# A gated linear attention layer and a channel-mixing layer on eight cores: one subtraction moved from VectorE to GpSimd, and three weight loads moved behind the first tile of phase B

## The reference

```python
# layer 1: a linear attention with a data-dependent decay
h = layernorm(x)
q = silu(h @ Wq.T);  f = sigmoid(h @ Wk.T);  v = h @ Wv.T
log_f = log_sigmoid(f);  k = 1 - f                      # 8 heads of 128
S_t = exp(log_f_t)[:, None] * S_{t-1} + k_t[:, None] * v_t[None, :]
o_t = q_t @ S_t
x = x + layernorm(rmsnorm(o, norm_w) @ Wo.T)
# layer 2: token shift, then a gated feed-forward
h = layernorm(x);  hp = h shifted by one token
xr = mu_r*h + (1-mu_r)*hp;  xk = mu_k*h + (1-mu_k)*hp
x = x + layernorm(sigmoid(xr @ W_r) * (square(relu(xk @ W_k)) @ W_v))
```

## Time and profile before

| | us |
|---|---|
| median of 2 runs | 5861.55 (5776.55 and 5946.55) |
| the profiled execution | 5770.28 |
| its span on core 1, the slowest | 5768.7 |
| spans of the 8 cores | 5745.9 to 5768.7 |

### The profile page before, as it was taken

The page is one execution under the profiler, slowest core; times in us unless marked ns, Lnnn a source line. Parts: engine busy times, 40 slices in busy tenths (PEclk is TensorE's granted clock), DMA queues, the critical chain, the costliest instruction groups (busy, mean ns, idle before and its releaser), DMA issues.

```text
span 5768.7 us, 65821 instructions; the slowest of 8 cores (5745.9 to 5768.7 us)
## 1 busy us (share of the span) xinstructions
PE 3475.0 (60%) x26608; PEld 2614.8 (45%) x26608; DVE 1992.9 (35%) x1978; ACT 1060.8 (18%) x1597; POOL 448.2 (8%) x205
## 2 busy tenths in 40 slices
PE   0566666666666666662056667666567666656665
PEld 0344444444444444441044455544445554444554
DVE  1333333333333333344123323333332323333233
ACT  0222222222222222221011111111111111111110
POOL 1111101100100111111310000000000000000000
PEclk9877777777777777776578888888778887778887
DMA  2000000000000000001210000000000000000000
GB/s 81 26 14 14 15 15 15 15 15 15 15 15 15 15 15 15 15 8 44 76 33 15 23 23 1 23 23 22 23 22 23 1 23 23 23 23 23 23 6 10
DMA packets 114736, 121.83 MB, mean 21 GB/s; under 512 B 3683, under 2 KB 107270, under 8 KB 114438
## 3 DMA queue, kind: packets, MB, share of 16 engines
q1 hardware_dynamic: 114438, 117.63, 6.5%
HBM read 83.00 MB, written 34.62 MB: 20 GB/s over the span
## 4 chain that ended last, share of the span: by engine, by line
PE 53%; DVE 26%; ACT 7%; DMA 6%; issue 5%; POOL 3%; DVEq 1%; ACTq 0%; POOLq 0%; SPq 0%
PE p_pj L250 39%; PE p_st L231 4%; PE p_pj L400 4%; DVE b_sb L329 3%; PE p_O L514 1%; PE p_O L531 1%; DVE r_a L207 1%; DMA outT<-x_sb 1%; ACT ebq L361 1%; DMA oB<-o_scr 1%; DVE p_A L457 1%; PE p_A L479 1%; DVE A_l L462 1%; DVE A_h L460 1%; POOL ebk L349 1%
## 5 line engine op out<-in xcount | busy, mean ns | idle before, releaser
L250 PE MATMUL p_pj<-o_pair,woh 128*128 128x256 bf16 x2176 | 414.6, 298 | 537.8 <-POOL o_pair L763 310.6
L250 PEld LDWEIGHTS p_pj<-o_pair,woh 128*128 128x128 bf16 x2176 | 228.7, 106 | 596.4 <-issue 553.2
L231 PE MATMUL p_st<-x_sb,onesc 128*1 128x256 f32 x544 | 172.2, 487 | 473.1 <-ACT oB L897 268.8
L250 PE MATMUL p_pj<-ln_h,wkh 128*128 128x256 bf16 x1088 | 311.9, 287 | 199.3 <-DVE ln_l L613 199.3
L250 PE MATMUL p_pj<-xk_h,wv2h 128*128 128x256 bf16 x1088 | 309.6, 285 | 125.0 <-DVE xk_l L821 125.0
L250 PE MATMUL p_pj<-o_pair,wol 128*128 128x256 bf16 x1088 | 322.3, 296 | 0.0
L231 PEld LDWEIGHTS p_st<-x_sb,onesc 128*1 128x1 f32 x544 | 53.3, 101 | 591.1 <-issue 560.3
L250 PE MATMUL p_pj<-xr_h,wrh 128*128 128x256 bf16 x1088 | 297.7, 274 | 24.8 <-DVE xk_l L938 24.8
L250 PE MATMUL p_pj<-ln_l,wkh 128*128 128x256 bf16 x1088 | 311.7, 287 | 0.0
L250 PE MATMUL p_pj<-ln_h,wkl 128*128 128x256 bf16 x1088 | 310.7, 286 | 0.0
L250 PE MATMUL p_pj<-xk_l,wv2h 128*128 128x256 bf16 x1088 | 309.7, 285 | 0.0
(11 more groups left out here) (176 smaller groups left out, 7903.5 us busy)
## 6 DMA issues: line engine op xcount, KB each, us to landing
x_sb<-xT SPq DMA_DIRECT2D x17, 1024.0 KB, 5.3
o_scr<-o_stage SPq DMA_DIRECT2D x68, 256.0 KB, 2.3
oB<-o_scr SPq DMA_DIRECT2D x17, 1024.0 KB, 5.4
xB<-xT SPq DMA_DIRECT2D x17, 1024.0 KB, 5.3
outT<-x_sb SPq DMA_DIRECT2D x16, 1024.0 KB, 4.5
wstage<-wkT SPq DMA_DIRECT2D x8, 512.0 KB
wstage<-wqT SPq DMA_DIRECT2D x8, 512.0 KB
wstage<-wvT SPq DMA_DIRECT2D x8, 512.0 KB
```

The source lines that it names most:

```text
L231: op("tensor", lambda e, ci=ci: e.matmul(p_st[0:1, 0:TILE], onesc[:], x_ap[:, ci, :], start=(ci == 0), stop=(ci == NCH - 1)), wait=wv if c ...
L250: e.matmul(bank[:, 0:TILE], wop[:, ci, dj * 128:(dj + 1) * 128], xop[:, ci, :], start=first, stop=last),
```

## The change

It has three parts.

1. In `load_split_weight` the load of a chunk waits for the count of the splitting engine only, and each weight's first chunk is made to wait for the last split of the weight before it (`first_wait`).
2. In `a_prep` the subtraction that makes kt_l goes from VectorE to GpSimd. It waits for ScalarE's kt_h, and all that needs kt now waits for GpSimd's count.
3. In phase B the loads of Wr, Wk2 and Wv2 are written behind the whole round of tile 0 (`b_load_wo(0)`, `b_aobc(0)`, `b_x2(0)`, `b_ln2_xrxk(0)`), which needs Wo only, and ahead of round 1. All queues follow this order: the 24 loads stand in SyncE's queue behind the load of xB for tile 1 and ahead of oB of tile 1.

```diff
@@ load_split_weight
-            wv = [("V", C["V"]), ("G", C["G"])] + (list(first_wait) if ci == 0 else [])
+            wv = [(E, C[E])] + (list(first_wait) if ci == 0 else [])
@@ phase A
-    ev_wq = load_split_weight(w_in["wqT"], wA["wqh"], wA["wql"], eng="gpsimd")
-    ev_wv = load_split_weight(w_in["wvT"], wA["wvh"], wA["wvl"], eng="vector")
+    ev_wq = load_split_weight(w_in["wqT"], wA["wqh"], wA["wql"], first_wait=[ev_wk],
+                              eng="gpsimd")
+    ev_wv = load_split_weight(w_in["wvT"], wA["wvh"], wA["wvl"], first_wait=[ev_wq],
+                              eng="vector")
@@ a_prep
-        op("vector", lambda e, par=par: e.tensor_tensor(kt_l[:, par], ebk[:], kt_h[:, par],
+        op("gpsimd", lambda e, par=par: e.tensor_tensor(kt_l[:, par], ebk[:], kt_h[:, par],
                                                         ALU.subtract),
-           wait=[ev_kth, ev_ktmul, ("V", C["V"])], inc=[("V", 1)])
-        ev_kt = ev("V")
+           wait=[ev_kth, ("G", C["G"])], inc=[("G", 1)])
+        ev_kt = ev("G")
@@ phase B
-    ev_wr = load_split_weight(w_in["wrT"], wB["wrh"], wB["wrl"], eng="gpsimd")
-    ev_wk2 = load_split_weight(w_in["wk2T"], wB["wk2h"], wB["wk2l"], eng="vector")
-    ev_wv2 = load_split_weight(w_in["wv2T"], wB["wv2h"], wB["wv2l"], eng="gpsimd")
@@ the loop of phase B
-    for it in range(nt + 1):
+    b_load_wo(0)
+    b_aobc(0)
+    b_x2(0)
+    b_ln2_xrxk(0)
+    bld.flush()
+    ev_wr = load_split_weight(w_in["wrT"], wB["wrh"], wB["wrl"], first_wait=[ev_wo],
+                              eng="gpsimd")
+    ev_wk2 = load_split_weight(w_in["wk2T"], wB["wk2h"], wB["wk2l"], first_wait=[ev_wr],
+                               eng="vector")
+    ev_wv2 = load_split_weight(w_in["wv2T"], wB["wv2h"], wB["wv2l"], first_wait=[ev_wk2],
+                               eng="gpsimd")
+    bld.flush()
+    for it in range(1, nt + 1):
```

## The result

The changed kernel takes 0.992 of the time of the kernel before, with a 95% interval of 0.9897 to 0.9943. The medians are 5958.21 us (27 runs) and 5952.33 us (26 runs). They hide the difference, because in most executions of either kernel some cores ran at a lower clock for a time; the ratio leaves those executions out. The profiled execution took 5725.16 us, where that of the kernel before took 5770.3 us.

The account below looks back on a forecast made before the run. It blamed TensorE's gaps (60% busy): serial weight loads and splits between phases, VectorE's path in phase A. 5770.3 - 22.6 (part 2) - 17.8 (part 3), part 1 0.0, gave 5730 us; range 5705 to 5785, upper end extended to 5825.

Parts of the forecast that it names:

- The range: Whole kernel: 5705 to 5785 us for executions like the profiled one, upper end stretched to 5825 for a median over runs.
- The sum itself: Whole kernel: 5770.3 us less 22.6 (part 2) and 17.8 (part 3) gives 5730 us, for executions like the lower run.
- The term of VectorE's path: Phase A, second chunk of each tile: removing kt_l from VectorE saves 1.33 us, 17 times, 22.6 us.
- rival B: Phase A: kt_l's move gives nothing, VectorE's PSUM readers are held, 10 us lost, 5762 us in all; chance 0.12.
- TensorE 1.3 us earlier in each tile: Phase A: a sign expected in the changed profile, TensorE starting 1.3 us earlier in every tile.
- contention: Phase B, Wr's splits beside tile 0's VectorE work: GpSimd loses 6.5 us over three chunks, bounds 0 and 18.5 us.
- xB's place in it: Phase B, SyncE's queue: tile 1's xB load goes ahead of Wr's first chunk, estimated to cost 3 us.
- rival A: Phase B: nothing contends and xB costs nothing, so part 3 gains 27 us, 5720 us in all; chance 0.15.
- Rival C: Phase B: Wr's splits are held and tile 1 comes no sooner, only part 2 remains, 5748 us; chance 0.08.
- the two terms with TensorE in them: Phase B: 49.24 us from tile 0's o split to x2(0), 33.8 us from tile 1's o split to row mean.
- one core's trace can stand for all: Whole kernel: cores span 5745.9 to 5768.7 us with nearly one clock, so one trace was used for all.
- rival D: TensorE restarts spend longer at the lower clock: 44 us per 0.01 of mean clock, 5804 us at 0.78; chance 0.06.

Follow-up runs that it names:

- e8: The kernel before with only the changed waits of the weight loads (splitting engine only, previous weight as first wait); span 5762.7 us against 5755.9, in one execution.
- e1: The kernel before with kt_l moved to GpSimd only in each tile's second chunk; no ratio, phase A 15 to 19 us shorter on the cores named.
- e2: The kernel before with kt_l moved to GpSimd only in each tile's first chunk; 1.0085 of the time before (1.005 to 1.0119).
- e10: The kernel before with only the first chunk's kt_l on GpSimd, a repeat of e2; no ratio, mean span 5778.0 us, 0.4% longer than before.
- e11: The kernel before with only the second chunk's kt_l on GpSimd, a repeat of e1; 0.9969 of the time before (0.9895 to 1.0042).
- e9: The kernel before with all of kt_l moved to GpSimd and nothing else; 0.9957 of the time before (0.9876 to 1.0037).
- e4: The changed kernel with Wr's load ahead of tile 1's xB; whole time not comparable, 234.7 us from Wo's last split to tile 1's row mean.

## Why the prediction was right, and where it was wrong

**The range** is the step that failed. It was made for a median over runs, and the measured median, 5958 us, lies 133 us above its upper end. To get from the sum to a median the prediction took the distance of two runs, 170 us apart: "a median over runs that scatter that way can be some 85 us higher", so 5825. Over 26 runs the unchanged kernel has a median of 5952.33 us, 91 us above that of the two, and 15 of the 26 took over 5900 us; so did 16 of the 27 of the changed kernel. A median of such a set lies among the long executions, and the step from the quick execution of the trace to it is 5958 - 5725 = 233 us, not 85. Two runs say little of where the median of many lies, and the profile of one execution says nothing of it. No run here shows why the long executions are the commoner ones. The sum itself, 5730 us, was given for executions like the profiled one, and the next such execution took 5725.16 us. That it is so near is in part luck: part 2 gave 2.8 us less than forecast and part 3 5.0 us more.

**Part 1**, 0 us forecast: e8 shows nothing else.

**Part 2**, 22.6 us forecast, 19.8 measured (19.6 alone). The term of VectorE's path was right: 1.33 us in the second chunk of a tile, 23.6 us in all 17 with the two longer tiles. VectorE's PSUM readers are not held by GpSimd's kt_l, vt_h stays at 0.69 us, and kt_l takes 2.46 us as its median on core 1, inside the 2.1 to 2.7 forecast. With that, rival B falls. TensorE's idle time fell by nearly as much, 21.8 us. But the sign "TensorE 1.3 us earlier in each tile" was wrong: most tiles kept their length, and 2.0 us came back as busy time. The remaining 1.8 us I can't place.

**Part 3**, 17.8 us forecast, 22.8 measured as a mean of the cores (22.2 alone), 26.6 on core 1. On core 1, from Wo's last split end to the row mean, step by step:

```
                                 forecast   measured
tile 0's o split                     6.2        6.9
to x2(0)                            49.2       45.6
Wr, first chunk                      7.2        6.8
Wr's splits                         53.4 }     58.6
contention                           6.5 }
Wk2                                 47.9       46.2
Wv2                                 57.2       58.0
tile 1's o split                     6.2        6.2
projection, statistics              33.8       30.3
sum                                267.5      258.7
```

The order in SyncE's queue, xB's place in it and the contention came as forecast. GpSimd lost 1.9, 1.5 and 2.6 us in the third, fourth and fifth chunk, 6.0 together, where 2.1, 1.7 and 2.7 were laid out; the stretch as a whole grew by 58.6 - 53.4 = 5.2 us. So rival A, nothing contends, falls, though the gain is nearly what it gave. Rival C falls by the row mean itself. What was mis-sized are the two terms with TensorE in them, 3.6 us to x2(0) and 3.5 us to the row mean. Both are the same cause, seen in windows from the o split's end to the row mean. First the kernel before, tile 0 (its last 10 us), then the changed kernel, tile 0 (its last 6.1 us); the columns are length, busy us of PE, PEld, DVE, ACT and POOL, clock, DMA:

```profile
2922.00:2932.00 10.00, 6.51 (x24) 1.85 (x24) 0.26 (x1) 2.30 (x2) 0.00 (x0) 0.66 0.00 1
```

```profile
2730.90:2737.00 6.10, 3.61 (x24) 1.30 (x24) 0.06 (x1) 1.91 (x1) 0.00 (x0) 1.00 0.00 0
```

The same 24 statistics matmuls ran at 0.66 of the full clock in the kernel before and at 1.00 in the changed one. The duration of 33.8 us, used twice, was copied from a stretch in which the clock happened to fall, as if it belonged to the work. The other seven cores of the same trace show it: they took 29.8 to 31.5 us from the o split's end to the row mean. So the step "one core's trace can stand for all" failed here. The first 8 us of the two projections, by contrast, run at 0.65 and 0.71, part of the time at the lower level in both.

**The clock**, rival D: means of 0.799 to 0.804 against 0.797 to 0.800, a move of 0.004 in the mean of the cores, and upward. As means of the cores, TensorE's busy time grew by 2.0 us in phase A and by 4.3 us from tile 1's row mean on, far less than D needs. What the clock did decide is which tiles got shorter.

## What to carry to other kernels

Look for the stretch in which the busiest engine does nothing and ask what one turn of its loop costs: here a chunk waited 3.7 to 4.2 us for its load before 1.9 or 3.2 us of work. Moving such a loop beside other work brought 23 us, a second and third buffer for it 178 us more; with the splits on the right engine besides, it is 230 us below the changed kernel.
Moving work from VectorE to GpSimd pays where VectorE is on the path and what follows reads PSUM; next to VectorE instructions on SBUF, both are held up, so add the hold to whichever is on the path.
Here time taken off VectorE's path came off TensorE's idle time over the phase, but not off each tile; count idle and busy time over the whole phase before you multiply a term by the number of tiles.
Compare stage by stage over all cores when the expected difference is below 1%; the whole time can carry terms that have nothing to do with the edit.

## What the runs showed of the hardware that was not expected

In e1, e2, e10 and e11, which move half of kt_l, the rest of phase B (from tile 1's row mean) took 2780 us as the mean over the cores in e1, e2 and e10 (each core of e2 and e10 within some 6 us of it) and 2797.9 us in e11, where cores 2 and 3 took 2839 and 2846. The kernel before, the changed kernel and e9 have 2753 to 2756, the other kernels 2760 to 2768, but for e4 with its lower clock (2812.7). The work of phase B from there on is the same in all of them. Most tiles of phase B, from one xr_l to the next, come in two lengths, under 168.1 us and 169.4 us or more. The kernel before has 1 to 3 long ones on a core, the changed kernel 1 to 6, e10 and e2 8 to 11. Windows at the same place in a short and in the long tile behind it, e10, core 6 (length, busy us of PE, PEld, DVE, ACT, POOL, clock, DMA):

```profile
3495.70:3503.70 8.00, 5.16 (x40) 2.49 (x38) 0.00 (x0) 2.29 (x2) 0.00 (x0) 1.00 0.00 0
3663.50:3671.50 8.00, 5.15 (x32) 2.08 (x30) 0.00 (x0) 2.29 (x2) 0.00 (x0) 0.82 0.00 0
3552.60:3560.60 8.00, 8.00 (x59) 6.49 (x60) 0.85 (x2) 0.00 (x0) 0.00 (x0) 0.79 0.01 2
3720.40:3728.40 8.00, 6.59 (x40) 5.06 (x41) 1.58 (x2) 0.00 (x0) 0.00 (x0) 0.61 0.01 2
```

The same instructions meet a granted clock of 1.00 and of 0.82 in the first pair, 0.79 and 0.61 in the second; a share between 0.50 and 1.00 is a window that was partly at 1.2 and partly at 2.4 GHz. Both windows are at places where TensorE starts again after a wait. The long tile has 8 fewer matmuls in the first window and 19 fewer in the second. From tile 1's row mean on, TensorE is busy for 1804.6 us in e10 and for 1782.4 in the kernel before, and idle for 975.1 and 972.4. So 22 of the 25 us are busy time, and the mean span of e10 came to 5778.0 us, 22 above the kernel before, with a phase A that is 1.7 us shorter. It is what rival D described, in kernels that it wasn't forecast for. Why these four fall into the long tiles and the whole change doesn't is open. I have no run that tells it.
